# The second feed-forward's filling steps ahead of attention's last steps in a macaron layer

## The chip, the cores and the metric

One core of a Trainium2 chip runs the whole program. The metric is the device time of one execution in microseconds (us). TensorE (PE) multiplies matrices, VectorE (DVE), ScalarE (ACT) and GpSimd (POOL) work element by element, and SyncE (SP) issues all the DMAs. Each runs its own list of instructions in order and waits on semaphores for the others.

## The reference

The input x has 16 sequences of 1024 rows of 256 numbers. Three blocks follow one another, each behind a layer norm and added to x:

```python
x = x + 0.5 * ffn(layernorm(x))
x = x + attn(layernorm(x))
x = x + 0.5 * ffn(layernorm(x))
```

The feed-forward quantizes its input and its weights to four-bit floats in blocks of 16 (`q = GRID[searchsorted(MID, |x/scale|)] * sign * scale` with `scale = max|x| / 6`), multiplies by the gate and up matrices (256 to 704 columns each), takes `silu(gate) * up`, quantizes that again and multiplies by the down matrix. Attention is causal and linear: q and k go through `elu + 1`, the running sums of k x v and of k along the sequence give numerator and denominator for each of 16 heads, then come a projection and a layer norm with gamma and beta.

## The kernel before

The rows of x are cut into N = 128 tiles of 128 rows, which stay in on-chip memory (SBUF) from the first block to the last. Each of the three blocks is a software pipeline. A step has a function for each engine, and step i does for various tiles the stage that is due: in the feed-forward (`ffn`, L590), TensorE's step i does gate/up of tile i and down of tile i - 4; ScalarE's the means of tile i + 6, the normalized x part of `hx` of tile i + 5, silu of tile i, and the two rounding passes `quarter` and `odd` of round i - 1; VectorE's the product `hx` of tile i, the block maxima, scales and quotients `y` of a round (the h part of tile i and the x part of tile i + 4 in one instruction), the last rounding `q` of round i - 1; GpSimd's the `rstd` and `shift` of tile i + 5 and the products that write `x_hl` of tile i + 2 and `h_hl` of tile i - 2; SyncE's the transposes of `x_hl` of tile i + 2 and of `h_hl` of tile i - 2. The second feed-forward therefore has filling steps -6 to -1, in which only the x parts are made; TensorE has nothing to do in them, and SyncE has its first transpose in step -2.

Attention's (`attention`, L927) step i is made the same way. TensorE's does q and k of tile i + 1, the transposed k of tile i, v of tile i + 1, the numerator (`num`) of tile i - 1, the scores and the state of tile i, and the projection (`ps_z`) of tile i - 2. So in step 129 TensorE has only the projection of tile 127, and in steps 130 and 131 nothing. SyncE's places v of tile i + 1 and transposes `o_hl` of tile i - 1 and `x_hl` of tile i + 3. GpSimd's makes the masked k (`k_even`, `k_odd`) of tile i, `o_hl` of tile i - 2, `mid` of tile i - 1, the `rstd` of tiles i + 3 and i - 3, and adds beta. VectorE's has the statistics of the projection of tile i - 3 (L1059), the mask, the add to x of tile i - 4 (L1073) and the outputs `o` of tile i - 1. ScalarE's has the high half of `o_hl` of tile i - 2, `q_feat` and `q_rows` of tile i, the exponentials of tile i + 1 and `k_nat` of tile i.

`stages` (L98) is the written-out order of the steps; every engine runs it with its own step functions. At the change from attention to the second feed-forward it interleaves seven rounds: attention's step 125 + k and then the feed-forward's step k - 6. After that the feed-forward goes on alone: steps 1 to 11 written out, then 13 turns of a loop of 8 steps, then the rest. The argument `ffn_ahead` sets where the first feed-forward's loop ends.

Within a step each engine waits only for what it needs. Three things make the step of one pipeline wait for the other pipeline: the buffers of the second feed-forward lie where attention's lie (`FFN_PLACES` and `ATTN_PLACES`, byte offsets in one area), so its first writers wait for attention's last readers; both use all eight banks of PSUM; and an engine's order is one list. The places that matter are `odd` of the second feed-forward at byte 27648, over attention's second `v_eo`, for which ScalarE waits in step -3 until the last numerator is done:

```python
if half == 1 and isinstance(i, int) and i == 1 - X_AHEAD:
    act.wait_ge(T["num_done"], N)
```

and `hx`, whose first two x parts wait for v and for k_odd of the last tiles (L832 to L834). On TensorE the first gate/up waits for the state and outputs of the last tile.

## Time and profile before

| | us |
|---|---|
| median of 3 runs | 2228.58 |
| lowest and highest run | 2224.03, 2229.47 |
| the profiled execution | 2227.84 |
| its span, first to last instruction | 2226.0 |
| TensorE, VectorE, ScalarE, GpSimd busy in it | 2120.2, 2060.1, 1849.7, 1897.2 |

The span is 1.84 us shorter than the profiled execution's own time. The mean granted TensorE clock over the span is 0.994 of full speed. A timeline row gives the start of an instruction in us from the span's start, its length, the engine, the line of the kernel, the operation, and in square brackets how long the engine was idle before it and what released it. The first feed-forward runs to about 750 us, attention from there to about 1500, the second feed-forward to the end.

### The profile page before, as it was taken

To read this page: it belongs to the slowest core of one execution; us is meant where nothing else is said; L and a number is where in the kernel's file an instruction comes from. 1 tells how busy PE (TensorE), PEld (TensorE's weight loads), DVE (VectorE), ACT (ScalarE), POOL (GpSimd) and SP (SyncE) were. 2 spreads that over 40 slices of the span, in tenths; PEclk is the share of its full clock that TensorE was granted. 3 is DMA by queue.
4 is the path that set the end of the run, shared out by engine and by line. 5 is a ranking of instruction groups with operands and counts; after the bars stand their busy time and mean duration, and the time that the engine had idled before them with its cause. 6 is when DMAs were issued, how large, how long until landed. Compare 5 with 4: busy or idle time off the path is not lost.

```text
span 2226.0 us, 90845 instructions
## 1 busy us (share of the span) xinstructions
PE 2120.2 (95%) x30384; PEld 1488.7 (67%) x30384; DVE 2060.1 (93%) x5231; ACT 1849.7 (83%) x3880; POOL 1897.2 (85%) x3002
## 2 busy tenths in 40 slices
PE   3899999999999899999999999969999999999998
PEld 1566666666666678888888888855656665666665
DVE  7999999999999689999999999978999999999997
ACT  7888888888888688888888888868888888888884
POOL 6899999999999677888888888868989999999996
PEclk9999999999999999999999999999999999999999
DMA  4765555555556433333333333324655555555555
GB/s 104 128 121 115 116 112 112 116 116 114 113 112 110 81 65 71 72 72 72 72 70 72 72 72 70 72 54 80 114 112 112 113 113 113 112 113 113 113 116 112
DMA packets 740337, 217.67 MB, mean 98 GB/s; under 512 B 670497, under 2 KB 740001, under 8 KB 740257
## 3 DMA queue, kind: packets, MB, share of 16 engines
q1 hardware_dynamic: 740256, 216.68, 48.2%
q8 instruction: 40, 0.66, 0.1%
q14 instruction: 41, 0.33, 0.0%
HBM read 20.38 MB, written 16.78 MB: 17 GB/s over the span
## 4 chain that ended last, share of the span: by engine, by line
DVE 38%; PE 20%; issue 12%; SPq 11%; POOL 11%; DMA 4%; DVEq 2%; ACT 1%; POOLq 0%; ACTq 0%
DVE ffn_y L748 10%; DVE ffn_per_block L717 8%; DVE ffn_hx L710 7%; PE ffn_ps_gu L860 6%; SPq L1028 5%; SPq L1034 4%; POOL ffn_h_hl L790 4%; POOL ffn_h_hl L791 4%; PE attn_ps_qk L1254 3%; DVE ffn_q L744 3%; PE ffn_ps_down L872 3%; DMA attn_xT<-attn_x_hl 3%; SPq L1040 2%; PE attn_ps_num L1293 2%; DVE ffn_scale L723 2%
## 5 line engine op out<-in xcount | busy, mean ns | idle before, releaser
L860 PE MATMUL ffn_ps_gu<-wgu_hi,ffn_xT 128*128 128x512 f16 (+1 forms) x3072 | 737.6, 363 | 17.7 <-DVE ffn_hx L710 7.5
L860 PEld LDWEIGHTS ffn_ps_gu<-wgu_hi,ffn_xT 128*128 128x128 f16 x3072 | 300.8, 98 | 303.6 <-issue 22.0
L806 ACT ACTIVATE ffn_quarter<-ffn_y,offsets 128x960 int16<-128x960 f32 (+2 forms) x264 | 282.6, 1071 | 185.0 <-DVE ffn_y L748 184.9
L860 PE MATMUL ffn_ps_gu<-wgu_lo,ffn_xT 128*128 128x512 f16 (+1 forms) x1536 | 431.0, 362 | 0.0
L872 PE MATMUL ffn_ps_down<-wd_hi,ffn_hT 128*128 128x256 f16 x2816 | 351.1, 273 | 18.9 <-DVE x_sb L737 13.6
L790 POOL TENSOR_TENSOR ffn_h_hl<-ffn_q,ffn_h_scale_hi 128x704 f16<-128x704 f16 x256 | 352.2, 1376 | 12.5 <-DVE ffn_h_scale_lo L754 8.4
L791 POOL TENSOR_TENSOR ffn_h_hl<-ffn_q,ffn_h_scale_lo 128x704 f16<-128x704 f16 x256 | 354.0, 1383 | 0.0
L872 PEld LDWEIGHTS ffn_ps_down<-wd_hi,ffn_hT 128*128 128x128 f16 x2816 | 265.7, 98 | 99.6 <-issue 37.0
L717 DVE TENSOR_REDUCE ffn_per_block<-ffn_hx 128x60 f32<-128x960 f32 (+2 forms) x264 | 298.4, 1130 | 21.3
L748 DVE TENSOR_TENSOR ffn_y<-ffn_hx,ffn_per_block 128x960 f32<-128x960 f32 (+2 forms) x264 | 295.3, 1119 | 0.0
L842 ACT ACTIVATE ffn_odd<-ffn_quarter,offsets 128x960 f16<-128x960 int16 (+2 forms) x264 | 278.7, 1056 | 10.5 <-POOL ffn_shift L783 10.5
L710 DVE SCALAR_TENSOR_TENSOR ffn_hx<-ffn_ps_gu,unscale,ffn_silu 128x704 f32<-128x704 f32 x256 | 243.2, 950 | 13.3 <-issue 9.5
L860 PEld LDWEIGHTS ffn_ps_gu<-wgu_lo,ffn_xT 128*128 128x128 f16 x1536 | 150.6, 98 | 155.0 <-issue 1.9
L801 ACT ACTIVATE ffn_silu<-ffn_ps_gu,unscale 128x704 f32<-128x704 f32 x256 | 212.0, 828 | 17.5 <-PE ffn_ps_gu L860 17.4
L781 POOL TENSOR_TENSOR ffn_x_hl<-ffn_q,ffn_x_scale_hi 128x256 f16<-128x256 f16 x256 | 157.8, 617 | 73.4 <-POOL ffn_rstd L773 37.4
L872 PE MATMUL ffn_ps_down<-wd_lo,ffn_hT 128*128 128x256 f16 x1536 | 210.2, 273 | 0.0
L1254 PE MATMUL attn_ps_qk<-attn_xT,attn_w_hi 128*128 128x128 f16 x2048 | 179.1, 220 | 18.4 <-DMA attn_xT<-attn_x_hl 15.8
L773 POOL TENSOR_TENSOR ffn_rstd<-ffn_rstd,minus_half 128x1 f32<-128x1 f32 x256 | 167.5, 654 | 20.0
L785 POOL TENSOR_TENSOR ffn_x_hl<-ffn_q,ffn_x_scale_lo 128x256 f16<-128x256 f16 x256 | 159.9, 625 | 20.0
L872 PEld LDWEIGHTS ffn_ps_down<-wd_lo,ffn_hT 128*128 128x128 f16 x1536 | 150.6, 98 | 17.7
L1254 PEld LDWEIGHTS attn_ps_qk<-attn_xT,attn_w_hi 128*128 128x128 f16 x2048 | 132.7, 98 | 42.1 <-DMA attn_xT<-attn_x_hl 39.5
L1063 DVE TENSOR_TENSOR attn_scores<-attn_ps_sc,attn_causal 128x1024 f32<-128x1024 f32 x128 | 154.5, 1207 | 0.0
(183 smaller groups left out, 5081.5 us busy)
## 6 DMA issues: line engine op xcount, KB each, us to landing
attn_v_eo<-attn_v_nat SPq DMA_DIRECT2D x512, 34.0 KB, 1.9
x_sb<-in_L_attn_x SPq DMA_DIRECT2D x128, 128.0 KB, 2.5
out<-x_sb SPq DMA_DIRECT2D x128, 128.0 KB, 2.1
ffn_xT<-ffn_x_hl SPq DMA_TRANSPOSE x256, 2.4
ffn_hT<-ffn_h_hl SPq DMA_TRANSPOSE x256, 3.5
attn_xT<-attn_x_hl SPq DMA_TRANSPOSE x128, 2.4
attn_oT<-attn_o_hl SPq DMA_TRANSPOSE x128, 2.4
x_sb<-in_L_ffn_w_gate SPq DMA_DIRECT2D x2, 352.0 KB, 5.0
```

The costliest lines, as they stand in the source:

```text
L710: nc.vector.scalar_tensor_tensor(hx[par][:, 0:INNER], ps_gu[par][:, INNER:2 * INNER], unscale[:, 1:2], silu[:], ALU.mult, ALU.mult).then_i ...
L717: nc.vector.tensor_reduce(amax[:, blocks_in(front)], blocks(hx[par][:, front]), AXX, ALU.max, apply_absolute_value=True).then_inc(S["amax" ...
L748: nc.vector.tensor_tensor(blocks(y[:, front]), blocks(hx[par][:, front]), over_block(inv[:, at], at.stop - at.start), ALU.mult).then_inc(S ...
L773: nc.gpsimd.tensor_tensor(rstd[oth][:], rstd[oth][:], minus_half[:, 0:1], ALU.pow).then_inc(S["rstd"], 1)
L790: nc.gpsimd.tensor_tensor(blocks(h_hl[par][:, 0:INNER]), blocks(q[par][:, 0:INNER]), over_block(h_scale_hi[par][:], HB), ALU.mult)
L791: nc.gpsimd.tensor_tensor(blocks(h_hl[par][:, INNER:]), blocks(q[par][:, 0:INNER]), over_block(h_scale_lo[par][:], HB), ALU.mult).then_inc ...
L801: nc.scalar.activation(silu[:], ps_gu[par][:, 0:INNER], ACT.Silu, scale=unscale[:, 0:1]).then_inc(S["silu"], 1)
L806: nc.scalar.activation(quarter[:, back], y[:, back], ACT.Identity, bias=offsets[:, 0:1], scale=4.0 / HALF_MIN).then_inc(S["quarter"], 1)
L842: nc.scalar.activation(odd[:, back], quarter[:, back], ACT.Identity, bias=offsets[:, 1:2], scale=HALF_MIN / 4.0).then_inc(S["odd"], 1)
L860: last = nc.tensor.matmul(ps_gu[par][:, a:b], xT[par][:, c, :], w[:, k, a:b], start=(n == 0), stop=(n == len(terms) - 1))
L872: last = nc.tensor.matmul(ps_down[:, 0:D], hT[par][:, c, :], w[:, c, :], start=(n == 0), stop=(n == len(terms) - 1))
L1254: last = nc.tensor.matmul(ps_qk[:, col, :], w[:, col, k], aT, start=(n == 0), stop=(n == len(terms) - 1))
```

## The change

The seven rounds at the change are split. In rounds k = 0 and 1 attention's step stands first, as before. In rounds 2 to 6 the feed-forward's step k - 6 stands first and attention's behind it. Two engines have attention's step lag by `attn_late` rounds in them, SyncE by one and TensorE by two; the steps that are left over follow the seventh round. With the step functions as they are, that amounts to this. On VectorE, ScalarE and GpSimd the steps -4 to 0 of the feed-forward come each ahead of attention's 127 to 131. On SyncE the transpose of tile 0's x (step -2) comes ahead of that of tile 127's `o_hl` (attention's step 128). On TensorE the first gate/up comes ahead of the projection of tile 127.

`odd` of the second feed-forward moves from byte 27648 to 1664, where its h part lies over attention's transposed outputs `oT` and its x part over nothing of attention's. The wait of ScalarE's `odd` for the last numerator goes from step -3 and a wait for the last projection comes in step 1. `quarter`, which lies over the first `v_eo`, gets a wait in step -3 for the numerator of the last tile but one. GpSimd's first write of `x_hl`, which lies over the scores, gets a wait for the last numerator.

```diff
--- before.py
+++ after.py
@@ -95,7 +95,7 @@
 FIRST, DEPTH = 12, 6
 
 
-def stages(eng, N, ffn_0, attn, ffn_1, ffn_ahead=6):
+def stages(eng, N, ffn_0, attn, ffn_1, ffn_ahead=6, attn_late=0):
 
     first, ahead = FIRST, 4
 
@@ -110,9 +110,15 @@
     attn_end = loop_end(ahead, ahead + 1, ATTN_TURN)
     in_turns(eng, attn, ahead + 1, attn_end, ATTN_TURN)
     in_order(eng, attn, attn_end, N + ahead - 7)
-    for k in range(7):
-        attn(eng, N + ahead - 7 + k, (N + ahead - 7 + k) % 2)
+    for k in range(2):
+        attn(eng, N - 3 + k, (N - 3 + k) % 2)
         ffn_1(eng, k - 6, k % 2)
+
+    for k in range(2, 7):
+        ffn_1(eng, k - 6, k % 2)
+        if k - attn_late >= 2:
+            attn(eng, N - 3 + k - attn_late, (N - 3 + k - attn_late) % 2)
+    in_order(eng, attn, N + ahead - attn_late, N + ahead)
     in_order(eng, ffn_1, 1, first)
     in_turns(eng, ffn_1, first, loop_end(6, first, TURN), TURN)
     in_order(eng, ffn_1, loop_end(6, first, TURN), N + DEPTH)
@@ -193,7 +199,7 @@
                 ffn_step(sp, 8 + k, k % 2)
             of_ffn.drained(sp)
             of_attn.turned(sp)
-            stages(sp, N, ffn_step, of_attn_steps.sync, of_ffn_1.sync, 9)
+            stages(sp, N, ffn_step, of_attn_steps.sync, of_ffn_1.sync, 9, 1)
             sp.wait_ge(stored, 16 * N)
 
         @block.vector
@@ -277,7 +283,7 @@
             of_ffn.down_turned(pe)
             in_order(pe, ffn_step, 4, 5)
             in_order(pe, ffn_step, 5, FIRST)
-            stages(pe, N, ffn_step, of_attn_steps.tensor, of_ffn_1.tensor)
+            stages(pe, N, ffn_step, of_attn_steps.tensor, of_ffn_1.tensor, 6, 2)
 
 
 @dataclass
@@ -583,7 +589,7 @@
 
 FFN_PLACES = (ffn_places(hT=(0, 2816), h_hl=(5632, 8448), q=(11264, 13184), hx=(15104, 18944), y=22784, quarter=26624, odd=28544, silu=30464, xT=(33280, 34304),
                          x_hl=(35328, 36352), squares=(37376, 37888), scaled_x=38400, x_scale_hi=(38912, 38944), x_scale_lo=(38976, 39040)),
-              ffn_places(hT=(3712, 6528), h_hl=(9344, 12160), silu=14976, xT=(17792, 18816), x_hl=(19840, 20864), q=(21888, 23808), quarter=25728, odd=27648, y=29568,
+              ffn_places(hT=(3712, 6528), h_hl=(9344, 12160), silu=14976, xT=(17792, 18816), x_hl=(19840, 20864), q=(21888, 23808), quarter=25728, odd=1664, y=29568,
                          hx=(38272, 33408), squares=(42112, 42624), scaled_x=43136, x_scale_hi=(43648, 43680), x_scale_lo=(43712, 43776)))
 
 
@@ -778,6 +784,8 @@
                 round_ready(pool, "q", i - 2)
                 ready(pool, "x_scale_lo", tx)
                 turned_before(pool, "xT", tx, par)
+                if half == 1 and isinstance(tx, int) and tx == 0:
+                    pool.wait_ge(T["num_done"], N)
                 nc.gpsimd.tensor_tensor(blocks(x_hl[par][:, 0:D]), blocks(q[par][:, INNER:]), over_block(x_scale_hi[par][:], XB), ALU.mult)
             if valid(ts, N):
                 nc.gpsimd.tensor_scalar(shift[oth][:], neg_mean[oth][:], 16.0, rstd[oth][:], ALU.mult, ALU.mult).then_inc(S["shift"], 1)
@@ -803,6 +811,8 @@
 
                 round_ready(act, "y", i - 1)
                 round_freed(act, "odd", i - 1, 1)
+                if half == 1 and isinstance(i, int) and i == 1 - X_AHEAD:
+                    act.wait_ge(T["num_done"], N - 1)
                 nc.scalar.activation(quarter[:, back], y[:, back], ACT.Identity, bias=offsets[:, 0:1], scale=4.0 / HALF_MIN).then_inc(S["quarter"], 1)
             if valid(tm, N):
 
@@ -837,8 +847,8 @@
             if back:
                 round_ready(act, "quarter", i - 1)
                 round_freed(act, "q", i - 1, 1)
-                if half == 1 and isinstance(i, int) and i == 1 - X_AHEAD:
-                    act.wait_ge(T["num_done"], N)
+                if half == 1 and isinstance(i, int) and i == 1:
+                    act.wait_ge(T["proj_done"], N)
                 nc.scalar.activation(odd[:, back], quarter[:, back], ACT.Identity, bias=offsets[:, 1:2], scale=HALF_MIN / 4.0).then_inc(S["odd"], 1)
             if valid(tn, N):
                 nc.scalar.activation(hx[oth][:, INNER:], x_sb[:, tn, :], ACT.Identity, bias=shift[oth][:], scale=rstd[oth][:]).then_inc(S["xn"], 1)
```

## Rows read from the trace of the kernel before

**Rows 1.** Windows in both long loops: busy us by engine, granted clock, DMA

```profile
280.00:380.00 100.00, 99.82 (x648) 62.80 (x647) 94.54 (x240) 86.00 (x182) 91.61 (x130) 1.00 0.57 115
1740.00:1840.00 100.00, 98.98 (x635) 60.66 (x632) 95.46 (x234) 85.06 (x181) 90.30 (x128) 1.00 0.53 112
```

**Rows 2.** Windows at the start of the second feed-forward, same columns

```profile
1500.00:1505.00 5.00, 2.78 (x7) 1.05 (x8) 2.35 (x9) 1.95 (x7) 3.40 (x8) 0.50 0.14 28
1505.00:1510.00 5.00, 4.55 (x22) 2.02 (x21) 3.24 (x7) 4.94 (x11) 3.28 (x8) 0.98 0.26 52
```

**Rows 3.** Timeline of TensorE: start, length, operation, [idle before <- releaser]

```profile
1484.16 0.76 PE L1293 MATMUL attn_ps_num<-attn_v_eo,attn_scores 128*32 128x34 f32 x64 [1.65 <-ACT attn_q_rows L1195]
...
1497.54 0.40 PE L1330 MATMUL attn_ps_z<-attn_bout,attn_ones 128*128 128x256 bf16 x1 [4.70 <-DMA attn_oT<-attn_o_hl]
1497.72 1.06 PE L1333 MATMUL attn_ps_z<-attn_w_hi,attn_oT 128*128 128x256 f16 x4
...
1502.22 1.87 PE L860 MATMUL ffn_ps_gu<-wgu_hi,ffn_xT 128*128 128x512 f16 x4 [3.01 <-issue]
...
1507.87 1.04 PE L860 MATMUL ffn_ps_gu<-wgu_hi,ffn_xT 128*128 128x512 f16 x4 [0.45 <-DMA ffn_xT<-ffn_x_hl]
```

**Rows 4.** Timeline of ScalarE, 1482 to 1507

```profile
1482.84 1.07 ACT L1195 ACTIVATE attn_q_rows<-attn_expo,attn_of_pair_eps,attn_of_pair 128x256 f32<-128x256 f32 x2
...
1487.07 0.60 ACT L844 ACTIVATE ffn_hx<-x_sb,ffn_shift,ffn_rstd 128x256 f32<-128x256 f32 x1 [1.77 <-POOL ffn_shift L783]
...
1492.89 0.51 ACT L842 ACTIVATE ffn_odd<-ffn_quarter,offsets 128x256 f16<-128x256 int16 x1 [3.22 <-POOL ffn_shift L783]
...
1506.88 0.85 ACT L801 ACTIVATE ffn_silu<-ffn_ps_gu,unscale 128x704 f32<-128x704 f32 x1
```

**Rows 5.** Timeline of GpSimd, 1481 to 1508

```profile
1481.19 0.27 POOL L783 TENSOR_SCALAR ffn_shift<-ffn_neg_mean,ffn_rstd 128x1 f32<-128x1 f32 x1
...
1482.12 0.48 POOL L1145 TENSOR_SCALAR attn_k_eo<-attn_expo,attn_odd 128x256 f32<-128x256 f32 x1
...
1490.21 0.19 POOL L1171 TENSOR_TENSOR attn_rstd<-attn_mv,attn_eps 128x1 f32<-128x1 f32 x1 [1.04 <-DVE attn_mv L1075]
...
1491.67 0.19 POOL L771 TENSOR_TENSOR ffn_rstd<-ffn_var,eps 128x1 f32<-128x1 f32 x1
...
1496.86 0.19 POOL L771 TENSOR_TENSOR ffn_rstd<-ffn_var,eps 128x1 f32<-128x1 f32 x1
...
1498.80 0.62 POOL L785 TENSOR_TENSOR ffn_x_hl<-ffn_q,ffn_x_scale_lo 128x256 f16<-128x256 f16 x1
1501.21 0.19 POOL L1171 TENSOR_TENSOR attn_rstd<-attn_mv,attn_eps 128x1 f32<-128x1 f32 x1 [1.79 <-DVE attn_mv L1075]
...
1507.28 0.62 POOL L785 TENSOR_TENSOR ffn_x_hl<-ffn_q,ffn_x_scale_lo 128x256 f16<-128x256 f16 x1
```

**Rows 6.** Timeline of SyncE's queue: the transposes of the second feed-forward

```profile
1499.57 9.68 SPq L689 DMA_TRANSPOSE ffn_xT<-ffn_x_hl  x3
```

**Rows 7.** Timeline of VectorE, 1486 to 1513

```profile
1486.71 0.42 DVE L717 TENSOR_REDUCE ffn_per_block<-ffn_hx 128x16 f32<-128x256 f32 x1
...
1500.09 0.42 DVE L1059 BATCH_NORM_STATS2 attn_z_bn<-attn_ps_z 128x6 f32<-128x256 f32 x1
...
1505.90 0.48 DVE L1073 SCALAR_TENSOR_TENSOR x_sb<-attn_zg,attn_rstd,x_sb 128x256 f32<-128x256 f32 x1
1507.82 0.95 DVE L710 SCALAR_TENSOR_TENSOR ffn_hx<-ffn_ps_gu,unscale,ffn_silu 128x704 f32<-128x704 f32 x1 [1.44 <-ACT ffn_silu L801]
...
1510.71 0.16 DVE L729 TENSOR_SCALAR ffn_x_scale_hi<-ffn_per_block 128x16 bf16<-128x16 f32 x1
...
1512.38 0.95 DVE L710 SCALAR_TENSOR_TENSOR ffn_hx<-ffn_ps_gu,unscale,ffn_silu 128x704 f32<-128x704 f32 x1
```

**Rows 8.** VectorE's x_scale_lo in 280:480 and 1740:1940: busy us, mean ns

```profile
L751 DVE TENSOR_TENSOR ffn_x_scale_lo<-ffn_scale,ffn_x_scale_hi 128x16 f32<-128x16 f32 x37 | 6.3, 170 | 0.0
...
L751 DVE TENSOR_TENSOR ffn_x_scale_lo<-ffn_scale,ffn_x_scale_hi 128x16 f32<-128x16 f32 x36 | 10.9, 303 | 0.0
```


## The prediction

> **What bounds the kernel now.** In what follows A(n) is attention's step n, F(n) the second feed-forward's. I read the windows first. In 280 to 380 us and in 1740 to 1840 us TensorE is busy for 99.82 and 98.98 of 100 us, VectorE for 94.54 and 95.46 [rows 1]: the long loops are full, and code that the change doesn't touch runs there. Between the phases it is otherwise: in 1500 to 1505 TensorE is busy for 2.78 of 5 us at a granted clock of 0.50, and only from 1505 on are 4.55 of 5 busy at 0.98 [rows 2]. 0.50 is the lower of its two levels, 1.2 GHz; it had idled for 3.01 us before tile 0 of the second feed-forward, and for 4.70 us before attention's last projection [rows 3]. So the change plays for a few us in some 40.
>
> Next I read each engine in order of time through that stretch, for what ended each wait. TensorE's attention of tile 126 starts at 1484.16 on ScalarE's q_rows [rows 3, 4]. ScalarE's `odd` of tile 0 stands for 3.22 us, because ScalarE is in order and the shift it waits for is issued by GpSimd only behind A(128) [rows 4]. GpSimd in turn waits for VectorE's statistics: 1.04 us at 1490.21, 1.79 at 1501.21 [rows 5]. The last link is GpSimd's second x_hl product of tile 0, ending 1499.42, on SyncE the transpose at 1499.57, TensorE's first gate/up at 1502.22 [rows 3, 5, 6].
>
> **The sum, step by step.** Durations come from the one profiled execution (2227.84 us, span 2226.0; the median of three runs, 2228.58, is 0.74 above it, and the runs spread over 5.44 us).
>
> Step 1, F(-4) ahead of A(127). Its last ScalarE instruction (the x part of `hx` for tile 1) waits for k_odd of tile 127, which is in GpSimd's A(127), now behind GpSimd's F(-4). Such a step's add, power and shift take 1.2 us (1491.67 to 1492.89, where `odd` is let go) [rows 4, 5]. k_odd ended at 1482.60, so now 1483.8 [rows 5]. The hx part of 0.60 us [rows 4] runs 1483.9 to 1484.5, then come o_hi and q_feat, and q_rows starts at about 1485.1 in place of 1482.84: **2.3 us later** [rows 4]. TensorE waits for it (1.65 us before, in [rows 3]), so tile 126's `num`, and what follows it in A(127) on VectorE, is 2.3 later. VectorE's own part of F(-4) began right behind A(127) at 1486.71 [rows 7]; now it lies in VectorE's wait and costs nothing (it is the late `num` that covers it; without that, 1.4 us). VectorE ends A(127) at 1486.7 + 2.3 = 1489.0.
>
> Step 2, F(-3) ahead of A(128). VectorE does it from 1489.0 to 1490.6. The shift comes behind A(127) on GpSimd, at 1488.7, so `odd` of tile 0 runs near 1489.2 instead of 1492.89: the 3.22 us stall goes [rows 4]. That needs `odd` in its new place, since the old wait was for the last `num`. The added wait of `quarter`, for the `num` of tile 126 (1487.6), holds ScalarE for about 1 us, with the squares of tile 3 behind it; GpSimd wants those only in F(-2). Taken at nothing, at most 1 us.
>
> Step 3, F(-2) ahead of A(129). VectorE enters A(128) at 1490.6, not 1488.1, so GpSimd's rstd of A(128) moves from 1490.21 to 1492.8. From there to the next feed-forward step is 1.46 us (1490.21 to 1491.67), and from that step's start to the end of x_hl 2.56 (1496.86 to 1499.42) [rows 5]: x_hl of tile 0 ends at 1492.8 + 1.46 + 2.56 = 1496.8, **2.6 us earlier**. GpSimd's new wait for the last `num` (about 1493.4) is over by then: nothing. One SyncE step later (2.65 us, 1499.57 to 1502.22 [rows 3, 6]) TensorE's F(0) starts at 1499.6. On SyncE exactly one pair of DMAs changes places, the transposes of tile 0's x and of tile 127's o. The latter's data come at 1498.0, so neither waits.
>
> Step 4, TensorE. Its F(-5) to F(-1) and its last two attention steps are empty, so "two late" means one thing: gate/up of tile 0 goes ahead of the projection of tile 127. F(0) took 5.2 us (1502.22 to 1507.87, less 0.45) [rows 3], ends at 1504.8, and the projection, 1.24 us in the slow clock (1497.54 to 1498.78 [rows 3]) and about 1.0 here, at 1505.9. Before, it ended at 1498.8.
>
> Step 5, what queues behind it. VectorE's A(130) opens with the statistics of that projection: from 1500.09 to **1505.9**. GpSimd's rstd follows 1.12 us later (1500.09 to 1501.21 [rows 5, 7]): 1507.0. Behind it in GpSimd's order stand 1.46 and then F(0), 2.6: x_hl of tile 2 ends at 1511.1, where it ended at 1507.90 [rows 5]. VectorE's `hx` of tile 0 starts 1.5 us behind the statistics, 1507.4 for 1507.82 (silu is ready: a table load and 0.85 us [rows 4] from 1502.8 on). But its x_scale_hi needs that x_hl: 1511.15 for 1510.71 [rows 7]. From there to the `hx` of tile 1 were 1.67 us (1510.71 to 1512.38); now the add of tile 127 (0.48, before at 1505.90) lies in them [rows 7]: 1513.2 for 1512.38, 0.8 late. ScalarE's chain (the y of F(0), `quarter`, `odd`) is only 0.4 late, and VectorE's next round meets it, so I take about the middle of 0.4 and 0.8, 0.6. The transpose of tile 2 comes 3 us later than before, yet TensorE catches up: of F(0)'s 5.2 us, the 2.9 before 1505.1 were at 0.50, so at full clock a gate/up takes about 3.75 us, and the rounds that follow start 4.56 us or more apart on VectorE (1507.82 to 1512.38) [rows 7]. The wait of F(1)'s `odd` for the last projection is over by 7 us. **Sum: +0.6 us.** 2.6 us are won on the way to the first gate/up and given back on the way to the second `hx`.
>
> Where a price has no row: VectorE's wait for the projection lies between nothing (the projection slips into a gap; the 2.6 stay) and the whole of F(0) at 1.2 GHz, 2 x 3.75 = 7.5 us for 5.2 [rows 2, 3], +2.3. I take the value in between, since the gap before F(0) is as long as it was.
>
> A row bears on all of this at once. VectorE's x_scale_lo takes 170 ns in the first feed-forward's loop and 303 in the second's [rows 8]; in the second GpSimd's product runs beside it. The Trainium skill (SBUF — State Buffer, SBUF: two separate sides) says that a two-input VectorE operation and a GpSimd operation take a shared port in turn, each blocking the other for its whole length. By that rule the reordered steps, which bring additions on both engines side by side, could cost more than their rows say; the trace agrees as to x_scale_lo, and the sum goes by the rows.
>
> **The rivals.** First, **the lead is kept**: TensorE waits so little that the projection is off the path, or GpSimd and VectorE run F(0) before it matters. For it: both were often idle here, 1.79 and 1.44 us [rows 5, 7]. Against: one in-order step stands behind the other. 2227.8 - 2.6 = 2225.2.
>
> Second, **slower: the last projection at the low clock**. By my sum TensorE idles for some 2.8 us before the last `num` and 4.8 before F(0). If 0.50 holds to the end of F(0), the projection is out 2.3 us later and step 5 moves with it: 0.6 + 2.3 = +2.9, 2230.7. It decides from the point where F(0) takes over 5.2 us. For it: the clock had been 0.50 for all of 1500 to 1505 [rows 2].
>
> Third, **the loop's rhythm changes**. The entry into the loop is shifted against GpSimd, and if x_scale_lo runs in 170 ns as in the first phase, 104 rounds (13 turns of 8) win at most 104 x 0.133 = 13.8 us, at least the 0.84 us in 100 that TensorE was less busy [rows 1], over 580 us 4.9; I take 9: 2219. It could go the other way by as much, 2237. Against: each turn of the loop lines the engines up again, and its code is the same.
>
> Fourth, **nothing of it shows**: the change only moves idle time, 2227.8. My sum is not 1 us from that, and both are one case.
>
> **The numbers.** No change to 0.6 late: chance 0.52. Lead kept in whole or part: 0.24. Low clock: 0.14. Rhythm better 0.06, worse 0.04. A measurement of this kernel tells 0.3% (6.7 us) from no change at best. The likeliest gives 2227.84 + 0.6 = 2228.4. The range takes the first two rivals (2225.2, 2230.7) and half the spread of the runs, 2.7, on each side: 2222.5 to 2233.4, leaving out the rhythm. Faster by over 0.3%: 0.07 (rhythm, and a hundredth for a lead that grows); slower: 0.04; same: 0.89.
>
> **What would show it.** Right: q_rows of tile 127 near 1485.1; `odd` of tile 0 near 1489.2 with no 3 us stall; TensorE's F(0) near 1499.6; after it the projection, and VectorE idle for over 2 us before the bn_stats at 1505.9; the second `hx` near 1513. Wrong: an F(0) later than 1501, a second `hx` before 1511, x_scale_lo at 170 ns in 1740 to 1840, or a span outside 2220 to 2231.

## The result and the profile after

| | before | changed |
|---|---|---|
| median, us | 2226.95 (12 runs) | 2230.25 (12 runs) |
| lowest and highest run | 2223.11, 2229.47 | 2228.02, 2232.55 |
| the profiled execution, its span | 2227.84, 2226.0 | 2231.51, 2229.8 |
| mean granted clock | 0.994 | 0.992 |

The ratio is 1.0017, interval 1.0009 to 1.0025: a loss of 2.0 to 5.6 us, and the medians are 3.3 us apart. It is less than the 0.3% that I had taken for the finest difference a measurement can tell, but with twelve runs each the interval leaves out 1, and a repeat (`r_after` below) gave 1.0018. The forecast was +0.6.

The page of the changed kernel first, with the span and the busy time of each engine:

```profile
span 2229.8 us, 90845 instructions
...
PE 2127.0 (95%) x30384; PEld 1493.4 (67%) x30384; DVE 2059.3 (92%) x5231; ACT 1849.3 (83%) x3880; POOL 1900.8 (85%) x3002
```

The instruction counts are those of before. TensorE is busy for longer by the most, 2127.0 us for 2120.2; GpSimd's 1900.8 for 1897.2 is the other rise. As nothing was added, TensorE's instructions took longer.

The windows of the changed kernel: us from the span's start, length, then busy us of TensorE, its weight load, VectorE, ScalarE, GpSimd, then the granted clock, DMA share and GB/s. The first row answers to the second of [rows 1], the next two to [rows 2], the last two tell where the clock is low in addition.

```profile
1740.00:1840.00 100.00, 98.97 (x634) 60.59 (x633) 96.03 (x236) 85.22 (x182) 90.25 (x129) 1.00 0.53 112
1500.00:1505.00 5.00, 2.58 (x7) 0.94 (x8) 2.58 (x9) 1.95 (x7) 3.83 (x9) 0.50 0.26 54
1505.00:1510.00 5.00, 5.00 (x25) 2.53 (x24) 1.47 (x6) 4.33 (x9) 0.47 (x1) 0.79 0.13 26
1487.00:1493.00 6.00, 5.39 (x135) 4.58 (x135) 3.06 (x13) 3.42 (x10) 3.35 (x8) 0.50 0.12 25
1515.00:1520.00 5.00, 2.17 (x6) 0.80 (x7) 4.86 (x13) 4.42 (x10) 2.65 (x6) 0.73 0.27 54
```

The long loop is as it was (98.97 us of 100 on TensorE, 98.98 before). At the change it isn't: 1505 to 1510 is at 0.79 (0.98 before), 1487 to 1493 is at half clock, 1.2 GHz, and so is a part of 1515 to 1520 (0.73).

TensorE's timeline in the changed kernel, columns as in [rows 3]. L1303 is the numerator, L1343 the projection, L870 gate/up:

```profile
1487.61 1.14 PE L1303 MATMUL attn_ps_num<-attn_v_eo,attn_scores 128*32 128x34 f32 x64 [3.99 <-ACT attn_q_rows L1205]
...
1495.26 0.76 PE L1303 MATMUL attn_ps_num<-attn_v_eo,attn_scores 128*32 128x34 f32 x64 [2.09 <-DVE attn_scores L1073]
...
1502.42 1.86 PE L870 MATMUL ffn_ps_gu<-wgu_hi,ffn_xT 128*128 128x512 f16 x4 [4.81 <-issue]
...
1504.93 1.91 PE L870 MATMUL ffn_ps_gu<-wgu_hi,ffn_xT 128*128 128x512 f16 x4
...
1507.28 0.81 PE L870 MATMUL ffn_ps_gu<-wgu_hi,ffn_xT 128*128 128x384 f16 x4
...
1508.26 0.27 PE L1340 MATMUL attn_ps_z<-attn_bout,attn_ones 128*128 128x256 bf16 x1
...
1517.83 1.89 PE L870 MATMUL ffn_ps_gu<-wgu_hi,ffn_xT 128*128 128x512 f16 x4 [5.08 <-DMA ffn_xT<-ffn_x_hl]
...
1522.81 1.03 PE L870 MATMUL ffn_ps_gu<-wgu_hi,ffn_xT 128*128 128x512 f16 x4
```

The numerator of tile 126 comes behind 3.99 us of idle time and takes 1.14 us where it took 0.76. Gate/up of tile 0 starts at 1502.42 behind 4.81 us of idle time, and the projection gets its turn 5.84 us later, at 1508.26. Before, the clock came back in the middle of tile 0's gate/up (its second group of four took 1.28 us), here near its end (1.91). That place is not fixed for a kernel: in the repeats the same group took 1.58 us (`r_before`) and 1.40 (`r_after`, where gate/up of tile 0 took 5.15 us in all). Gate/up of tile 2 then waits 5.08 us for its transpose and begins at half clock again: 4.98 us to the next one.

ScalarE and GpSimd, the rows that answer to [rows 4] and [rows 5]:

```profile
1486.28 1.07 ACT L1205 ACTIVATE attn_q_rows<-attn_expo,attn_of_pair_eps,attn_of_pair 128x256 f32<-128x256 f32 x2
...
1489.56 0.51 ACT L816 ACTIVATE ffn_quarter<-ffn_y,offsets 128x256 int16<-128x256 f32 x1 [1.84 <-PE attn_ps_num L1308]
...
1491.00 0.49 ACT L852 ACTIVATE ffn_odd<-ffn_quarter,offsets 128x256 f16<-128x256 int16 x1
...
1498.94 0.51 ACT L852 ACTIVATE ffn_odd<-ffn_quarter,offsets 128x256 f16<-128x256 int16 x1 [3.91 <-POOL ffn_shift L791]
```

```profile
1498.99 0.62 POOL L793 TENSOR_TENSOR ffn_x_hl<-ffn_q,ffn_x_scale_lo 128x256 f16<-128x256 f16 x1
...
1510.34 0.19 POOL L1181 TENSOR_TENSOR attn_rstd<-attn_mv,attn_eps 128x1 f32<-128x1 f32 x1 [4.87 <-DVE attn_mv L1085]
...
1513.76 0.62 POOL L793 TENSOR_TENSOR ffn_x_hl<-ffn_q,ffn_x_scale_lo 128x256 f16<-128x256 f16 x1
```

VectorE, answering to [rows 7]:

```profile
1491.63 0.30 DVE L1126 TENSOR_TENSOR attn_first<-attn_ps_kT_first,attn_own 128x136 f32<-128x136 f32 x1 [1.18 <-PE attn_ps_v_second L1331]
...
1509.22 0.43 DVE L1069 BATCH_NORM_STATS2 attn_z_bn<-attn_ps_z 128x6 f32<-128x256 f32 x1 [2.99 <-PE attn_ps_z L1343]
...
1516.58 0.94 DVE L716 SCALAR_TENSOR_TENSOR ffn_hx<-ffn_ps_gu,unscale,ffn_silu 128x704 f32<-128x704 f32 x1
...
1523.01 0.95 DVE L716 SCALAR_TENSOR_TENSOR ffn_hx<-ffn_ps_gu,unscale,ffn_silu 128x704 f32<-128x704 f32 x1 [1.46 <-PE ffn_ps_gu L870]
```

The `odd` of tile 0 no longer stands (1491.00). The next one does, for 3.91 us, as its like did before (3.13). The statistics of the last projection come at 1509.22, GpSimd's rstd behind them has waited 4.87 us, and tile 2's x_hl is ready at 1514.38 where it was at 1507.90. The `hx` of tile 1 and of tile 2 start at 1516.58 and 1523.01, the latter behind 1.46 us of waiting for the slow gate/up.

**A yardstick.** Traces are some us apart before the change even begins, though the code up to there is the same. So I compare kernels by the distance from the start of VectorE's first state product of tile 126 (`attn_first`, 1481.67 before, 1482.78 changed) to the start of `hx` of tile 11, the last step written out before the loop. It is 83.46 us before and 87.60 changed: **+4.14**. In all traces of this study the start of it lies between 1479.84 and 1483.79, and from the start of that `hx` to the end of the span it is 658.3 to 660.9 us, in no order that goes with the kernels. Relative times below are from that start.

### The profile page after: what moved, and what is told of

Its sections match the earlier page's. It is cut to its first block, busy times and chain, and to the rows that moved or that the text cites. A ratio compares the mean times of both kernels' runs of the same rounds, so it can differ in the third digit from the quotient of the medians.

```text
span 2229.8 us, 90845 instructions
## 1 busy us (share of the span) xinstructions
PE 2127.0 (95%) x30384; PEld 1493.4 (67%) x30384; DVE 2059.3 (92%) x5231; ACT 1849.3 (83%) x3880; POOL 1900.8 (85%) x3002
## 4 chain that ended last, share of the span: by engine, by line
DVE 42%; PE 21%; issue 12%; SPq 11%; POOL 6%; DMA 4%; DVEq 2%; ACT 1%; POOLq 0%; ACTq 0%
DVE ffn_y L754 10%; DVE ffn_per_block L723 10%; DVE ffn_hx L716 8%; PE ffn_ps_gu L870 6%; SPq L1038 5%; SPq L1044 4%; PE attn_ps_qk L1264 4%; DVE ffn_q L750 3%; PE ffn_ps_down L882 3%; DMA attn_xT<-attn_x_hl 3%; SPq L1050 2%; DVE ffn_scale L729 2%; PE attn_ps_num L1303 2%; POOL ffn_h_hl L798 2%; POOL ffn_h_hl L799 2%
## 5 line engine op out<-in xcount | busy, mean ns | idle before, releaser
L870 PE MATMUL ffn_ps_gu<-wgu_hi,ffn_xT 128*128 128x512 f16 (+1 forms) x3072 | 741.7, 364 | 19.0 <-DMA ffn_xT<-ffn_x_hl 7.3
L870 PEld LDWEIGHTS ffn_ps_gu<-wgu_hi,ffn_xT 128*128 128x128 f16 x3072 | 301.7, 98 | 307.3 <-issue 25.1
L870 PE MATMUL ffn_ps_gu<-wgu_lo,ffn_xT 128*128 128x512 f16 (+1 forms) x1536 | 433.1, 364 | 0.0
L870 PEld LDWEIGHTS ffn_ps_gu<-wgu_lo,ffn_xT 128*128 128x128 f16 x1536 | 151.1, 98 | 156.7 <-issue 4.7
```

What stands on the lines that cost most here:

```text
L870: last = nc.tensor.matmul(ps_gu[par][:, a:b], xT[par][:, c, :], w[:, k, a:b], start=(n == 0), stop=(n == len(terms) - 1))
```

## The experiments

My theory after the two traces was that two parts of the change cost, each by itself: the late q_rows (early split) and the late projection, and that both act through TensorE's low clock. The rivals: the order of the steps alone is to blame, whatever the clock; the new place and its waits cost; or VectorE's waits do.

| run | ratio, 95% interval | first of 127 | x_hl 0 | stats 127 | hx 1 | distance |
|---|---|---|---|---|---|---|
| before | 1 | 4.83 | 17.13 | 18.42 | 30.71 | 83.46 |
| r_before | 0.9998 [0.9989, 1.0006] | 4.72 | 17.03 | 18.33 | 30.62 | 83.36 |
| changed | 1.0017 [1.0009, 1.0025] | 8.85 | 16.21 | 26.44 | 33.80 | 87.60 |
| r_after | 1.0018 [1.0009, 1.0027] | 8.85 | 16.19 | 25.75 | 33.11 | 87.88 |
| e1 | 1.0004 [0.9995, 1.0013] | 8.35 | 15.70 | 22.85 | 33.26 | 85.67 |
| e2 | 1.0009 [1.0000, 1.0018] | 4.83 | 14.50 | 23.98 | 31.33 | 86.33 |
| e3 | 1.0000 [0.9991, 1.0009] | 4.80 | 14.47 | 21.62 | 30.79 | 83.19 |
| e4 | 0.9996 [0.9987, 1.0005] | 4.82 | 17.12 | 19.10 | 31.58 | 84.32 |
| e5 | 1.0016 [1.0007, 1.0025] | 13.09 | 20.23 | 28.58 | 35.94 | 88.33 |
| e6 | 1.0001 [0.9992, 1.0010] | 4.83 | 14.50 | 28.41 | 31.48 | 83.91 |
| e7 | 1.0008 [0.9999, 1.0017] | 8.83 | 16.17 | 30.12 | 33.19 | 85.63 |
| e8 | 0.9992 [0.9983, 1.0001] | 7.15 | 14.85 | 23.27 | 30.62 | 82.85 |
| e9 | 1.0039 [1.0026, 1.0053] | 6.27 | 18.56 | 28.61 | 41.89 | 94.61 |
| e10 | 0.9991 [0.9983, 1.0000] | 5.85 | 15.51 | 29.77 | 31.25 | 83.70 |
| e11 | 0.9993 [0.9984, 1.0002] | 4.83 | 17.13 | 18.42 | 30.71 | 83.45 |
| e12 | 0.9992 [0.9983, 1.0001] | 4.83 | 14.51 | 28.17 | 29.65 | 82.12 |
| e13 | 1.0008 [0.9999, 1.0017] | 7.14 | 14.59 | 25.17 | 32.52 | 86.44 |
| e14 | 0.9995 [0.9986, 1.0004] | 8.53 | 15.87 | 24.37 | 31.72 | 83.96 |

The distance is 83.46 and 83.36 in the two traces of the kernel before and 87.60 and 87.88 in those of the changed kernel; I had expected the repeats to stay within 0.9 and 0.7 us. The ratio of each is to the kernel before, run on the same chip in between. The columns in the middle are relative start times: VectorE's first state product of tile 127, GpSimd's second x_hl product of tile 0, the statistics of the last projection, `hx` of tile 1.

**e1, e2, e3: undo one part, the other, both.** From the changed kernel:

```diff
-            stages(pe, N, ffn_step, of_attn_steps.tensor, of_ffn_1.tensor, 6, 2)
+            stages(pe, N, ffn_step, of_attn_steps.tensor, of_ffn_1.tensor, 6, 1)
```

is e1. The split one round later is e2, and e3 has both edits:

```diff
-    for k in range(2):
+    for k in range(3):
...
-    for k in range(2, 7):
+    for k in range(3, 7):
...
-        if k - attn_late >= 2:
+        if k - attn_late >= 3:
```

> The changed kernel, but TensorE's lag is one round and not two, so that its first gate/up stands behind the projection of tile 127 again; all else as changed. Theory (the projection behind the first gate/up holds VectorE and GpSimd, whose x_hl of tile 2 then lets TensorE idle for 5 us and fall to the low clock): the statistics of the projection at about 1505 instead of 1509.2, x_hl of tile 2 done at about 1511.5 instead of 1514.4, no idle of 5 us before the third gate/up; 2.5 to 4 us faster than the changed kernel, ratio to before 1.0000 to 1.0006. Rival (the late q_rows of tile 127, which lets TensorE idle 4 us and drops the clock at 1486.8, is what costs): unchanged, 1.0017; by it the low clock still stretches tile 126 and the gate/up waits longer, for the projection.

> The changed kernel with the split one round later: step -4 of the feed-forward stands behind attention's 127 again on all engines, -3 to 0 stand first as changed, and the first gate/up still stands ahead of the last projection. Rival (late q_rows costs): TensorE no longer idles 4 us for q_rows, the clock stays up through tile 126, and the loss goes; ratio to before about 1.000. Theory (the place of the projection costs): VectorE still idles for 3 us before the projection's statistics and TensorE 4 to 5 us before the third gate/up; ratio 1.0010 to 1.0017.

> The changed kernel with the later split and the projection ahead of the first gate/up: only steps -3 to 0 go ahead of attention's 128 to 131 on VectorE, ScalarE and GpSimd. Both theories: as fast as before or faster, since the stall of 3.2 us before `odd` of tile 0 is gone and nothing is late: ratio 0.9988 to 1.0000. If a lead of a step in itself is worth nothing, 1.0000.

The statistics of the last projection came 22.85 us from the anchor in e1, and the ratios are within 0.0001 of what the theory had. Each part costs by itself, and nothing is left when both are undone. The projection's place costs 1.93 us of distance (changed to e1) or 3.14 (e2 to e3), the early split 1.27 (changed to e2) or 2.48 (e1 to e3). The smaller of these, and all the steps of the early split in the ratios, are no larger than the scatter of one trace and the intervals; they count because each comes twice with one sign and because the late start shows in the third column. e3 tells a second thing. Its x_hl of tile 0 is 2.66 us earlier than before, as I had forecast for the change, and its distance is shorter by 0.27, which is no more than the scatter. TensorE in e3:

```profile
1482.36 0.83 PE L1303 MATMUL attn_ps_num<-attn_v_eo,attn_scores 128*32 128x34 f32 x64 [1.54 <-DVE attn_scores L1073]
...
1490.72 1.14 PE L1303 MATMUL attn_ps_num<-attn_v_eo,attn_scores 128*32 128x34 f32 x64 [5.16 <-DVE attn_scores L1073]
...
1499.67 0.39 PE L1340 MATMUL attn_ps_z<-attn_bout,attn_ones 128*128 128x256 bf16 x1 [5.50 <-DMA attn_oT<-attn_o_hl]
```

It stands 5.16 us before the last numerator and 5.50 before the last projection: what one end is given, the other waits for. Both came behind that at half clock (1.14 and 0.39 us). As far as e3 goes, the lead that the whole change is built on is worth nothing that can be told.

**e4: the new place and its waits alone,** in the order of before (SyncE and TensorE without their lag).

```diff
-    for k in range(2):
-        attn(eng, N - 3 + k, (N - 3 + k) % 2)
-        ffn_1(eng, k - 6, k % 2)
...
+    for k in range(7):
+        attn(eng, N + ahead - 7 + k, (N + ahead - 7 + k) % 2)
+        ffn_1(eng, k - 6, k % 2)
```

> The kernel before with its own order, but `odd` at byte 1664 and the changed waits (quarter for the numerator of tile 126, odd in step 1 for the last projection, x_hl for the last numerator). Both theories: no difference from before, 1.0000 within 0.0007. Another account (the place or the waits cost) has 1.001 or more.

The ratio contains 1. The distance is 0.86 longer. Two links are late in the trace. The last projection waited 6.05 us for its transposed input (4.70 in [rows 3]) and started at 17.39 us from the anchor for 15.87, though that transpose was issued in the same place; what held it is not shown. And gate/up of tile 0 started where it did before, at 20.53, but the clock came back later in it (its second group of four took 1.91 us for 1.28), so it took 6.36 us for 5.2. Neither is a wait that was moved, so I take a distance as good to about 0.9 us, and the place and the waits cost nothing that can be told. e9 and e10 below show that one trace can be off by more, 1.0 to 1.4 us.

**e5: fill TensorE's gaps with matmuls,** whose sums nothing reads: 34 in A(127), 40 ahead of F(0)'s gate/up, 30 ahead of F(2)'s.

> The changed kernel with extra matmuls of 256 columns into free banks where TensorE idles: 34 in attention's 127 ahead of the wait for q_rows (idle 3.99 us), 40 ahead of the second feed-forward's tile 0 (4.81 us) and 30 ahead of its tile 2 (5.08 us). Their sums are never read. Distance: from VectorE's attn_first of tile 126 to the 12th `hx` product of the second feed-forward, 87.60 us in the changed kernel, 83.46 before. Rival now (the order only costs because the idle time lowers the clock, and the clock stretches gate/up 0 to 5.84 us and gate/up 2): granted clock 1.00 throughout, gate/up 0 in about 3.75 us, the projection's statistics 2 us sooner, distance 84.0 to 85.0. Theory (the waits themselves cost, one engine behind the other): distance 86.5 or more.

A miss of its own making. TensorE in e5:

```profile
1486.48 6.21 PE L1303 MATMUL attn_ps_v_second<-attn_bout,attn_ones 128*128 128x256 bf16 x34 [3.77 <-POOL attn_mid L1172]
1492.62 0.77 PE L1314 MATMUL attn_ps_num<-attn_v_eo,attn_scores 128*32 128x34 f32 x64
```

The first group stood behind the wait for `mid`, so it came after the gap and not into it, and the numerator started 10.75 us from the anchor for 4.83 in the changed kernel, 5.9 late. Distance and ratio are those of the changed kernel. Yet from x_hl of tile 0 to the end the path took 88.33 - 20.23 = 68.10 us, against 71.39 in the changed kernel: 3.3 less, with the clock up. That asked for a better placed try, e8.

**e6, e7: take VectorE's waits away.** On VectorE, GpSimd and ScalarE attention's steps 130 and 131 go behind F(0); e6 with the later split, e7 with the change's. The edit of e6, on top of that of e2 (`held` is 5 on the three engines, 7 on the others):

```diff
-        if k - attn_late >= 3:
+        if k - attn_late >= 3 and k < held:
...
-    in_order(eng, attn, N + ahead - attn_late, N + ahead)
+    in_order(eng, attn, N + ahead - attn_late - 7 + held, N + ahead)
```

> The changed kernel with the later split, and on VectorE, ScalarE and GpSimd attention's steps 130 and 131 behind step 0 of the feed-forward, so that what needs the last projection no longer stands ahead of what the third gate/up needs. Theory: the wait of 3 us on VectorE and 5 us on GpSimd goes, TensorE doesn't idle 5 us before tile 2, first `hx` product at about 23 us from attn_first of tile 126 (26.15 before, 25.46 with the later split alone); distance to the 12th `hx` product 81 to 82.5 (83.46 before), ratio to before 0.9990 to 0.9997. Rival (the steps in order are bound by the clock or by a cycle of their own): 83.2 to 84, ratio 1.0000.

> As the run with the steps held back, but with the split of the change (step -4 ahead of attention's 127, so q_rows of tile 127 is late by 2.3 us again). Theory: distance 1.2 to 2.5 us above that run, since the late q_rows has a price of its own; ratio to before 0.9997 to 1.0005. If q_rows is covered once the projection is out of the way: the same distance.

Against e2 and the changed kernel the distance falls by 2.42 and 1.97, so part of the price of the late projection is what queues behind its statistics. But e6 missed what the theory had (81 to 82.5 us, a ratio under 0.9997) and came out where the rival had it. The wait only moved on by a tile. GpSimd's rstd of attention there, and TensorE's gate/up of tile 3:

```profile
1512.20 0.19 POOL L1181 TENSOR_TENSOR attn_rstd<-attn_mv,attn_eps 128x1 f32<-128x1 f32 x1 [6.04 <-DVE attn_mv L1085]
```

```profile
1519.02 1.89 PE L870 MATMUL ffn_ps_gu<-wgu_hi,ffn_xT 128*128 128x512 f16 x4 [4.66 <-DMA ffn_xT<-ffn_x_hl]
```

e7 to e6, 1.72 us, is the early split's price once more, as expected; the ratio of e7, 1.0008, is above the 1.0005 that I had allowed.

**e8: the gaps filled in the right places.** The fillers of A(127), 30 of them, stand ahead of all waits of the numerator:

```diff
+            if isinstance(i, int) and i == N - 1:
+                pe.wait_ge(S["v_nat"], N)
+                pe.wait_ge(S["kv_second"], N - 1)
+                for _ in range(30):
+                    nc.tensor.matmul(ps_v, ones3[:], bout3[:], start=True, stop=True)
...
+                if half == 1 and isinstance(tg, int) and tg in (0, 2):
+                    if tg == 2:
+                        freed(pe, "silu", tg, 2)
+                        freed(pe, "h", tg, 2)
+                    for _ in range({0: 40, 2: 24}[tg]):
+                        nc.tensor.matmul(ps_gu[1 - tg // 2][:, 0:D], wd_hi[:, 0, 0:P], wgu_hi[:, 0, 0:D], start=True, stop=True)
```

> The changed kernel with extra matmuls on TensorE, whose sums are never read: 30 in A(127) ahead of the waits for the last numerator but one, 40 ahead of F(0)'s gate/up and 24 ahead of F(2)'s. They keep the engine busy where it idled for 3.99, 4.81 and 5.08 us. If the low clock is what the later second gate/up and the 4.1 us cost: the granted clock stays at 1.00 from about 1487 on, F(0) takes 3.8 us and not 5.8, and the distance from the first attention output of tile 126 on VectorE to the hx of tile 11 falls from 87.6 and 87.9 to 84 to 85.5 us; time ratio near 1.0003. If the order of the engines' steps alone is the cause: the distance stays at 86.5 or more and the ratio near 1.0015.

TensorE in e8:

```profile
1482.21 3.44 PE L1292 MATMUL attn_ps_v_second<-attn_bout,attn_ones 128*128 128x256 bf16 x30
1486.34 0.76 PE L1314 MATMUL attn_ps_num<-attn_v_eo,attn_scores 128*32 128x34 f32 x64 [0.70 <-ACT attn_q_rows L1211]
...
1495.87 4.57 PE L869 MATMUL ffn_ps_gu<-wgu_hi,wd_hi 128*128 128x256 f16 x40
1500.27 1.03 PE L876 MATMUL ffn_ps_gu<-wgu_hi,ffn_xT 128*128 128x512 f16 x4
...
1503.84 0.27 PE L1351 MATMUL attn_ps_z<-attn_bout,attn_ones 128*128 128x256 bf16 x1
...
1513.23 1.04 PE L876 MATMUL ffn_ps_gu<-wgu_hi,ffn_xT 128*128 128x512 f16 x4 [0.91 <-DMA ffn_xT<-ffn_x_hl]
...
1516.81 1.03 PE L876 MATMUL ffn_ps_gu<-wgu_hi,ffn_xT 128*128 128x512 f16 x4
```

Not one step of the order is other than in the changed kernel, and the engine has more to do. It is 0.25% faster than the changed kernel (0.9992 for 1.0017, each beside the kernel before; their intervals are apart), and more than I had expected (1.0003, a distance of 84 to 85.5). Gate/up of tile 0 leads to the projection in 3.57 us, and tile 2's takes 3.58. The distance is 4.75 and 5.03 us shorter than in the two traces of the changed kernel. The filling is not complete: the numerator of tile 127 and the projection behind it still ran at half clock (1.13 and 0.39 us). With its gate/ups at full clock this order costs nothing that can be told; the loss needs the low clock.

**e9: the swap alone in the kernel before.** TensorE's attention steps 129 to 131 go behind F(0), the other engines stay as they were.

```diff
-        attn(eng, N + ahead - 7 + k, (N + ahead - 7 + k) % 2)
+        if not (swapped and k >= 4):
+            attn(eng, N + ahead - 7 + k, (N + ahead - 7 + k) % 2)
         ffn_1(eng, k - 6, k % 2)
+    if swapped:
+        in_order(eng, attn, N + 1, N + ahead)
```

> The kernel before with one thing changed: on TensorE the last projection stands behind the first gate/up. VectorE and GpSimd still have A(130), which opens with that projection's statistics, ahead of F(-1). If the late projection is a wait that every later x_hl stands behind, it is worse here than in the changed kernel, since tile 1's x_hl also stands behind it: distance 88.5 to 91.5 us (83.5 before), ratio 1.0025 to 1.004. If only the split and the two together cost, the distance is under 86 and the ratio under 1.001.

GpSimd and VectorE in e9:

```profile
1509.95 0.19 POOL L1174 TENSOR_TENSOR attn_rstd<-attn_mv,attn_eps 128x1 f32<-128x1 f32 x1 [10.56 <-DVE attn_mv L1078]
```

```profile
1508.82 0.43 DVE L1062 BATCH_NORM_STATS2 attn_z_bn<-attn_ps_z 128x6 f32<-128x256 f32 x1 [8.68 <-PE attn_ps_z L1336]
```

Here the reordering of the other engines is needed: without it, tile 1's x_hl stands behind the last projection too, and GpSimd is idle for 10.56 us. The distance was worse than I had it (94.61, expected 88.5 to 91.5), the ratio as expected. TensorE also idled 9.08 us before F(0) and 7.82 before F(1), and both began at half clock. 1.44 us of the distance were there before any of it: in this trace the clock had fallen by the numerator of tile 126, behind 1.64 us of idle time (1.13 us for 0.76), and the first product of tile 127 is at 6.27 for 4.83.

**e10: the tail spread.** The split one round later, the projection behind F(0), and on VectorE the order F(0), A(130), F(1), A(131), F(2); on GpSimd and ScalarE F(0), F(1), A(130), A(131) (`tail` is 1 and 0). The part of the edit that spreads the tail:

```diff
...
+        in_order(eng, attn, N + 2, N + 2 + tail)
+        in_order(eng, ffn_1, 1, 2)
+        in_order(eng, attn, N + 2 + tail, N + ahead)
+        in_order(eng, ffn_1, 2, first)
...
```

> The split one round later, the projection behind the first gate/up as in the changed kernel, and attention's last two steps spread so that nobody waits for it: VectorE has F(0), A(130), F(1), A(131), F(2); GpSimd and ScalarE have F(0), F(1), A(130), A(131). If the late projection costs only by what queues behind its statistics: no GpSimd x product waits for it, the distance is 82 to 84 us and the ratio 0.999 to 1.0003. If the swap on TensorE costs by itself (low clock, PSUM banks), the distance is 85 us or more and the ratio about 1.001.

GpSimd in e10, tiles 2 and 3 and then attention's rstd:

```profile
1503.85 0.62 POOL L799 TENSOR_TENSOR ffn_x_hl<-ffn_q,ffn_x_scale_lo 128x256 f16<-128x256 f16 x1
...
1509.55 0.62 POOL L799 TENSOR_TENSOR ffn_x_hl<-ffn_q,ffn_x_scale_lo 128x256 f16<-128x256 f16 x1
1510.85 0.19 POOL L1187 TENSOR_TENSOR attn_rstd<-attn_mv,attn_eps 128x1 f32<-128x1 f32 x1 [0.68 <-DVE attn_mv L1091]
```

Nothing of the second feed-forward waits for the projection now, and though F(0) takes 6.04 us, most of it at half clock, the distance is that of before. It is so even with a start that was 1.02 us late by chance (5.85 in the third column, where e2, e3 and e6 with the same steps up to there have 4.80 to 4.83): the clock fell in the scores of tile 127, behind a wait of 1.65 us. So the order can be mended as well as the clock. With the steps behind the projection spread, its loss is gone though the low clock stays (distance 83.70 for 86.33 in e2).

**e11 to e14: is the clock the difference between the two kernels?** e11 fills the kernel before (14 in A(127), 20 ahead of the last projection, 24 ahead of F(0)), e12 fills e10 (14 and 26), e13 fills only the changed kernel's first gap, e14 only the two later ones. All use the two pieces of e8; new is e11's group ahead of the last projection:

```diff
+                if isinstance(to, int) and to == N - 1:
+                    pe.wait_ge(S["kv_first"], N)
+                    pe.wait_ge(S["o_ready"], N)
+                    for _ in range(20):
+                        nc.tensor.matmul(ps_v, ones3[:], bout3[:], start=True, stop=True)
```

> The kernel before, with extra matmuls on TensorE whose sums are never read: 14 in A(127) ahead of the waits for the numerator, 20 ahead of the last projection, 24 ahead of F(0)'s gate/up, filling idle times of 1.65, 4.70 and 3.01 us. The filled changed kernel had a distance of 82.85 us (87.6 and 87.9 unfilled) and a ratio of 0.9992. If the changed order loses to the old one by the clock, the old one gains much less from being filled: F(0) at full clock is worth at most 5.2 - 3.75 = 1.45 us, so the distance is 82 to 83 (83.4 unfilled), the ratio 0.9993 to 1.0000, and the two filled kernels are within 0.8 us of each other. If the clock costs both the same 4 to 5 us, the distance is 79 or less and the ratio 0.9985 or less, and the order is still to blame.

> The spread tail (split one round later, last projection behind the first gate/up, attention's last two steps spread between F(0) and F(2)) with 14 extra matmuls in A(127) and 26 ahead of F(0)'s gate/up, their sums never read. F(0) took 5.8 us there at the low clock; at full clock it takes 3.8. If TensorE's first gate/ups are on the path, the distance falls from 83.7 by 1.5 to 2 us to about 82 and the ratio from 0.9991 to about 0.998 to 0.9985. If VectorE and GpSimd hold the path there, nothing is gained: 83.5, 0.9991.

> The changed kernel with only the first 30 extra matmuls (in A(127), ahead of the waits for the numerator; their sums are never read). If the fall of the clock at 1487 is what costs: numerator, scores and state of tile 127 run at full clock, the first attention output of tile 127 is 1.7 us earlier (7.15 us behind the anchor, 8.85 without), and the distance is 85.5 to 86.5 us, ratio 1.0010. If the clock matters only at the gate/ups behind the projection, the distance stays at 87 to 88 and the ratio at 1.0015 to 1.0018.

> The changed kernel with only the 40 extra matmuls ahead of F(0) and the 24 ahead of F(2) (their sums are never read). F(0) takes 3.8 us for 5.8 and F(2) is at full clock: if that is the larger part, the distance is 84 to 85 us and the ratio 1.0000 to 1.0005; if the first gap's clock is the larger part, the distance is 86 or more.

TensorE in e11:

```profile
1494.89 2.78 PE L1343 MATMUL attn_ps_v_second<-attn_bout,attn_ones 128*128 128x256 bf16 x20
...
1500.35 2.78 PE L859 MATMUL ffn_ps_gu<-wgu_hi,wd_hi 128*128 128x256 f16 x24
1504.10 1.04 PE L866 MATMUL ffn_ps_gu<-wgu_hi,ffn_xT 128*128 128x512 f16 x4 [0.97 <-DMA ffn_xT<-ffn_x_hl]
...
1509.90 1.04 PE L866 MATMUL ffn_ps_gu<-wgu_hi,ffn_xT 128*128 128x512 f16 x4 [2.06 <-DMA ffn_xT<-ffn_x_hl]
```

F(0) runs at full clock in e11 and the distance stays at 83.45, so the gain is less than the 0.4 to 1.4 I had allowed. The 1.5 us that gate/up wins turn into a wait of 2.06 us for the next transpose (0.45 in [rows 3]). The old order had that cover all along, if a thin one: the 6.36 us of e4 were more than it holds. So being filled brings the changed kernel 4.8 to 5.0 us and the old one nothing that shows, and the two filled kernels stand at 0.9992 and 0.9993. e13 and e14 split it: 1.2 to 1.4 us for the first gap, 3.6 to 3.9 for the later ones, together about what e8 gave. How the 3.6 to 3.9 divide between gate/up of tile 0 and of tile 2 was not tried. e12 was expected at 0.998 to 0.9985 and came out at 0.9992. Its distance fell by 1.58, as if TensorE's path had been shortened, but 1.02 of that is the late start of e10's trace: from the first product of tile 127 on it is 77.29 us for 77.85, 0.56 less, though F(0) took 2.46 us less. That much could not show in the ratio, and most of the slow F(0) was covered there too.

e8, e10 and e12 each lie 0.0008 or 0.0009 below the kernel before with intervals that end at 1.0000 or 1.0001. So none of them is shown to beat it.

## Why the prediction was wrong

**Step 1** was right in its size and wrong in what it left out. q_rows was 2.33 us late (3.50 for 1.17), as forecast. I took that as a pure shift. But it stretched TensorE's wait from 1.65 us to 3.99, the clock fell, and the numerator, scores and state ran at 1.2 GHz: the first product of tile 127 came 4.02 us late and not 2.3. e13, with that gap filled, has it 2.31 late. What the step left out is worth 1.2 to 1.4 us of distance.

**Steps 2 and 3** held as orders. The stall of tile 0's `odd` went, and the added waits cost nothing (e4); `quarter` stood 1.84 us for the numerator, more than the 1 us of my bound; ScalarE's next `quarter` waited 1.20 us for VectorE's `y` all the same. x_hl of tile 0 was 0.9 us earlier and not 2.6, by step 1's miss: in e13 it is 2.54 earlier. F(0) started at 1502.42 where I had 1499.6 (1501.3 if the anchor is laid on that of the trace before), so my own sign of being wrong, an F(0) later than 1501, came true.

**Step 4** had a size that was not a constant. It gave F(0) the 5.2 us of the trace before, in which the clock returned 2.9 us into it. It took 5.84 and 5.15 in the two traces of the changed kernel and 6.19 in e13. At full clock it takes 3.57 (e8; my estimate was 3.75). My bound of 7.5 held, but what I chose inside it had no row behind it: a duration that holds a change of clock belongs to its place in one execution. This size did not decide, though: with F(0) at 5.15 us, what I had given it, the distance was 87.88.

**Step 5** is where the sum broke, at "yet TensorE catches up". I saw that tile 2's transpose would be 3 us late and priced the wait only by the length of the rounds behind it. It became 5.08 us of idle time (4.91 in `r_after`) and a second gate/up at half clock. That and the slow F(0) cost 3.6 to 3.9 us (e14). `hx` of tile 1 was 3.09 late (forecast 0.8), that of tile 11 4.14.

So the step of the prediction that failed is the clock as a term of steps 1 and 5: it stood at nothing, and the runs show it at 4.8 to 5.0 us of distance. Without it my sum of +0.6 was right to within the scatter: the changed order with its gaps filled is 0.5 to 0.6 shorter than before, hx of tile 1 within 0.1 us of it.

**The rivals.** The lead kept was wrong, and e3 tells why: there x_hl of tile 0 does come 2.66 us earlier, and the distance is 0.27 shorter. The second rival, the low clock at the last projection, had the right kind of cause, the side and nearly the time (2230.7; measured 2230.25). I gave it 0.14. That the time agrees is in part luck: it put the whole loss on F(0), and its sign, F(0) over 5.2 us, came true in one trace of the changed kernel (5.84) and not in the other (5.15), with the same loss in both. It saw one of the three places. The other two could be had from my own numbers: 1.65 us of waiting and 2.3 more make 3.95 ahead of the numerator of tile 126 (3.99 measured), and in step 5 a transpose 3 us late stands ahead of tile 2. The gap that I did name, 2.8 us before the last numerator, was 2.09, and that numerator ran at full clock (0.76 us). The rhythm stayed (x_scale_lo takes 308 ns in 1740 to 1940 of the changed kernel, 303 in [rows 8]). The three places add up to the whole loss, which leaves nothing that can be told for the order by itself.

The Trainium skill (TensorE: Matmul & The Clock Gate, Part 1: The HAM clock gate (the "warmup" mystery)) says that for modelling the ramp's price is under 1% of a typical kernel's span. The runs agree, 0.0025 from the changed kernel to e8, and that is more than the whole difference that was to be predicted.

## What to carry to other kernels

When a reordering moves a wait on TensorE, price the clock with the wait: take each stretch behind a new gap at both levels, and take a duration that straddles a rise of the clock for none of them. Then ask what stands behind the slow stretch: in the old order a slow first gate/up was all but covered by the next transpose, in the new one the last projection, VectorE, GpSimd and the next tiles stood behind it. A few matmuls whose sums nobody reads, placed ahead of every wait of the gap, are a cheap way to ask whether an order or its clock is to blame. And repeat the trace: where the clock rises and falls differs between two executions of one kernel, by 0.7 us in F(0) here.

## What was not expected of the hardware

The length of the idle time did not tell when the clock would fall. In the changed kernel the numerator behind 3.99 us took 1.14 us, at half clock. In e1 TensorE stood 3.96 us for q_rows, its numerator still took 0.76, and the scores 1.1 us later took 1.95 (1.05 at full clock, in e2):

```profile
1485.48 0.76 PE L1303 MATMUL attn_ps_num<-attn_v_eo,attn_scores 128*32 128x34 f32 x64 [3.96 <-ACT attn_q_rows L1205]
...
1486.57 1.95 PE L1316 MATMUL attn_ps_sc<-attn_q_rows,attn_k_eo 64*64 64x128 f32 x32
```

In e10 it fell behind a wait of only 1.65 us. The same wait in the kernel before and in e2 left the scores at full clock (1.05 us). The mean granted clock is 0.52 from 1484 to 1487:

```profile
1482.45 0.76 PE L1309 MATMUL attn_ps_num<-attn_v_eo,attn_scores 128*32 128x34 f32 x64 [1.65 <-ACT attn_q_rows L1211]
...
1483.42 1.89 PE L1322 MATMUL attn_ps_sc<-attn_q_rows,attn_k_eo 64*64 64x128 f32 x32
```

What decides between them was not tried. And adding 94 matmuls to a program in which TensorE is busy for 95% of the time made it faster, by 0.0025.
